# A decoder layer on one core: the output projection of batch 0 spread over the self-attention cycles in halves, and its transposed rows passed through a score bank

## The chip, the cores and the metric

One core of one Trainium2 chip runs the whole layer. The metric is the device time of one execution in microseconds; less is better. TensorE is called PE in the profile, VectorE DVE, ScalarE ACT, GpSimd POOL, and SP is the engine that issues the DMAs.

## The reference

```
x = layernorm(x + self_attention(x))      # 32 heads of 16, causal, ALiBi bias, softmax, output projection w_proj
x = layernorm(x + cross_attention(x, ctx))# 32 query heads of 128, 8 key/value heads, keys and values of ctx and of x
x = layernorm(x + grouped_ffn(x))         # 16 groups: 32 -> 128, gelu, 128 -> 32
```

x is 2 x 256 x 512 and ctx is 2 x 512 x 512, in float32. So there are 512 tokens of x in four tiles of 128, and for the keys and values of the cross-attention 1536 rows (1024 of ctx and 512 of x) in twelve tiles of 128. The tiles of ctx come first; those of x need the output of the first layer norm.

## The kernel before

Each product in full precision is made of three matmuls, hi x hi, hi x lo and lo x hi (`three_passes`, lines 48 to 50): whatever goes into such a product is split by ACT, which makes the hi part, and DVE (or POOL), which subtracts to get the lo part. The program has three stages. The change is in the first, `self_attention_and_keys`, which does the self-attention and, between its pieces, the key and value projections of the cross-attention.

The self-attention runs in 16 quads of four heads (8 quads for batch 0, then 8 for batch 1). A quad's scores, S, are one set of 16 small matmuls into banks 0 to 3, a bank for each head. E is a head's softmax: DVE adds the bias and takes the extreme (line 588, semaphore `s_out`), ACT makes the exponentials (448). R, for half a quad, is the reciprocals (DVE, 597), the scaling of the probabilities (POOL, 383 and 385) and the bias of the next quad (POOL, 378). T is a head's three transposes on PE (810) and their copy out by DVE (603). Every second quad, PV weighs the values with two quads of probabilities (822), and A splits the result: ACT (455), then DVE (609, semaphore `at_lo`).

The filler between these is the projection of the twelve row tiles. `part (n, r)` is a pair of the four contraction steps of a group, six matmuls of 128 x 512: each row tile n has 8, two for each of its four groups (keys 0, keys 1, values 0, values 1), and the groups take banks 5 and 6 in turn. ACT copies a key group out and squares it (478, 483), DVE sums the squares (626, 629), POOL scales the rows (411, 413), PE turns them (KT, 839) and ACT copies them out for the store (KX, 462). CT turns the rows of ctx (832).

At the end of a batch, Y is the output projection of a token tile in two halves of six matmuls each, into bank 5 or 6. LN is its sum with x and the statistics on DVE (672 to 678, semaphore `y_sum` after the sum) and a power on POOL (430). X1 normalises on DVE (686). XT turns the rows (PE 898, ACT 541, DVE 681, semaphore `x1t_lo`), and the key tiles 8 to 11 are projected from these.

The order of all this is one list, `order_of_work`, written out by hand: a loop over c, in the following called cycle c, which does S of quad c + 1, E and R of quad c + 1 and T of quad c. Every engine walks the same list and does its own share of each entry, so the list is the order on each engine. T, PV, CT, KT, XT and QT use banks 4 and 7 in turn (`RING`), so each of them waits (`drained`) until the last but one of them has been taken out.

On PE, cycles 8 to 14 read, with p for part:

```
8   S9 PV3 p5.0 T8.0 KT4.0 p5.1 Y0.0 Y0.1 Y1.0 Y1.1 T8.1 p5.2 T8.2 KT4.1 p5.3 T8.3 p5.4
9   S10 CT6 p5.5 T9.0 p5.6 T9.1 p5.7 XT0 T9.2 p6.0 XT1 T9.3 KT5.0 p6.1
10  S11 PV4 p6.2 T10.0 KT5.1 p6.3 T10.1 p6.4 T10.2 CT7 p6.5 T10.3 p6.6
11  S12 p6.7 T11.0 p7.0 T11.1 KT6.0 p7.1 T11.2 p7.2 T11.3
12  S13 PV5 KT6.1 p7.3 T12.0 p7.4 T12.1 p7.5 T12.2 p7.6 T12.3
13  S14 p7.7 T13.0 p8.0 T13.1 KT7.0 p8.1 T13.2 p8.2 T13.3
14  S15 PV6 KT7.1 p8.3 T14.0 p8.4 T14.1 p8.5 T14.2 p8.6 T14.3
```

On DVE, LN 0 stands between the copy of T8.1 and E9.2 in this list, LN 1 between the copy of T8.2 and E9.3.

Of the kernel before, what the change touches and what calls it, by code (L numbers as in the profile page):

```python
# [81 lines left out]
def order_of_work():  # L82

    order = [("S", 0), ("W", 5), ("V", 0), ("E", (0, 0)), ("V", 1), ("E", (0, 1)), ("V", 2), ("E", (0, 2)), ("CT", 0), ("CX", 0), ("V", 3),
             ("E", (0, 3)), ("R", (0, 0)), ("W", 6), ("R", (0, 1))]
    q = 0

    def parts(count):
        nonlocal q
        for _ in range(count):  # L90
            n, r = divmod(q, PARTS)
            if r in (1, 3) and n >= 1:
                order.append(("KT", (n - 1, r // 2)))
            if r == 5 and n + 1 < B * CT:
                order.append(("CT", n + 1))
            order.append(("part", (n, r)))
            if r in (1, 3) and n >= 1:
                order.append(("KX", (n - 1, r // 2)))
            if r == 5 and n + 1 < B * CT:
                order.append(("CX", n + 1))  # L100
            q += 1

    for c in range(NQ):
        more, pair, mid = c + 1 < NQ, c % 2 == 0 and c >= 2, c - NQ // 2
        if more:
            order.append(("S", c + 1))
        if pair:
            order.append(("PV", c // 2 - 1))
        for i in range(QUAD):
            if mid == 0 and i == 1:  # L110
                parts(q % 2)
                order += [("Y", (0, 0)), ("Y", (0, 1)), ("Y", (1, 0)), ("Y", (1, 1))]
            elif mid == 0 and i >= 2:
                order.append(("LN", i - 2))
                parts(1)
            elif mid == 1 and i < 2:
                order.append(("X1", i))
                parts(1)
            elif mid == 1:
                parts(1)  # L120
                order.append(("XT", i - 2))
            else:
                parts(2 if c == NQ - 1 and i == 0 else 1)
            if more:
                order.append(("E", (c + 1, i)))
            if pair and i == 0:
                order.append(("A", c // 2 - 1))
            if i == 3 and more:
                order.append(("R", (c + 1, 0)))
            order.append(("T", (c, i)))  # L130
        if c < NQ - 5:
            parts(1)
        if c == 3:
            order.append(("W", 7))
        if more:
            order.append(("R", (c + 1, 1)))
    parts(1)
    order += [("PV", NQ // 2 - 1), ("A", NQ // 2 - 1)]
    parts(1)
    order += [("Y", (2, 0)), ("Y", (2, 1))]  # L140
    parts(1)
    order.append(("LN", 2))
    parts(1)
    order += [("X1", 2), ("Y", (3, 0)), ("XT", 2), ("Y", (3, 1)), ("LN", 3)]
    parts(1)
    order.append(("W", 8))
    parts(1)
    order.append(("X1", 3))
    parts(2)
    order += [("Q", 0), ("XT", 3)]  # L150
    parts(1)
    order += [("Q", 1), ("QM", (0, 0))]
    parts(1)
    order.append(("QT", 0))
    parts(1)
    order += [("Q", 2), ("QT", 1)]
    parts(1)
    order += [("Q", 3), ("QM", (0, 1))]
    parts(1)
    order += [("W", 9), ("QM", (1, 0))]  # L160
    parts(1)
    order.append(("KS", 0))
    parts(1)
    for j in range(UT):
        order.append(("XS", j))
        parts(1)
        if j == 0:
            order.append(("QM", (1, 1)))
        order.append(("XM", j))
        if j > 0:  # L170
            order.append(("XI", j - 1))
        order.append(("XE", j))
    parts(1)
    order.append(("XI", UT - 1))
    parts(max(0, ROWS * PARTS - q))
    parts(4)
    order += [("XS", UT), ("XS", UT + 1)]
    parts(1)
    assert q == ROWS * PARTS + 5
    return order  # L180


def self_attention_and_keys(nc, d, k):

    with ExitStack() as ctx:
# [66 lines left out]
        GH = KVH // 2  # L252
        RING, GROUPS = (4, 7), (5, 6)
        before = {4: ("V", 0), 7: ("V", 3), 5: ("V", 1), 6: ("V", 2)}
        place = {}
        for what, a in ORDER:
            if what in ("T", "PV", "CT", "KT", "XT", "QT"):
                at = RING[sum(1 for e in place if e[0] in ("T", "PV", "CT", "KT", "XT", "QT")) % 2]
            elif what == "Y" and a[1] == 0 or what == "part" and a[1] % 2 == 0 and a[0] < ROWS:
                at = GROUPS[sum(1 for e in place if e[0] in ("Y", "part")) % 2]  # L260
            else:
                continue
            place[what, a] = at, before[at]
            before[at] = what, a

        def bank_of(what, a):
            if what == "part":
                a = (a[0], a[1] - a[1] % 2)
            elif what == "Y":
                a = (a, 0)  # L270
            return place[what, a][0]
# [162 lines left out]
        def _(act):  # L434
# [30 lines left out]
            def part(n, r):  # L465
                if r == 0 and n >= 1:
                    act.wait_ge(g_ps, 4 * n)
                    if n >= 2:
                        act.wait_ge(v_store, 16 * (n - 1))
                    nc.scalar.activation(v_st[:, GH:KVH, :].rearrange("p h e -> p (h e)"),  # L470
                                         bank[:, bank_of("part", (n - 1, 6)), :], ACT.Copy).then_inc(vg_late, 1)
                if r in (2, 4) and n < ROWS:
                    g = r // 2 - 1
                    w = slice(GH * g, GH * (g + 1))
                    act.wait_ge(g_ps, 4 * n + g + 1)
                    if n >= 1:
                        act.wait_ge(kt_ps, 2 * n + g - 1)
                    nc.scalar.activation(k_rows[:, w, :].rearrange("p h e -> p (h e)"),
                                         bank[:, bank_of("part", (n, 2 * g)), :], ACT.Copy).then_inc(kg_out, 1)
                    act.wait_ge(kg_out, 2 * n + g + 1)  # L480
                    if 2 * n + g >= 1:
                        act.wait_ge(kss_made, 2 * n + g)
                    nc.scalar.activation(k_sq[:], k_rows[:, w, :], ACT.Square).then_inc(ksq_made, 1)

            for j in range(TT):
                act.wait_ge(xt_ps, j + 1)
# [23 lines left out]
            for what, a in ORDER:  # L510
# [13 lines left out]
                elif what == "W":  # L524
# [7 lines left out]
                        act.wait_ge(q_ps, TT)  # L532
                    for i in range(KT):
                        weights_hi(a, i)
                elif what == "A":
                    attention_hi(a)
                elif what == "part":
                    part(*a)
                elif what == "XT":
# [25 lines left out]
        def _(dve):  # L565
# [87 lines left out]
            for what, a in ORDER:  # L653
# [15 lines left out]
                elif what == "LN":  # L669
# [6 lines left out]
                    nc.vector.bn_aggr(mv[:, a, :], stats[:, a, :]).then_inc(y_mv, 1)  # L676
                    dve.wait_ge(y_mv, a + 1)
                    nc.vector.tensor_scalar(var[:, a:a + 1], mv[:, a, 1:2], LN_EPS, None, ALU.add).then_inc(var_made, 1)
                elif what == "XT":
                    dve.wait_ge(x1t_hi, a + 1)  # L680
                    nc.vector.tensor_tensor(xT_lo[:, :, tokens(a)],
                                            bank[:, bank_of("XT", a), :].rearrange("p (k t) -> p k t", k=KT),
# [46 lines left out]
        def _(pe):  # L729
            def drained(what, a):  # L730

                held, i = place[what, a][1]
                if held == "V":
                    pe.wait_ge(v_out, 2 * (i + 1))
                elif held == "T":
                    pe.wait_ge(pt_out, QUAD * i[0] + i[1] + 1)
                elif held == "PV":
# [50 lines left out]
            def scores(c):  # L788
# [2 lines left out]
                keys = kT_odd if odds else kT_even  # L791
                if c >= 1:
                    pe.wait_ge(s_out, QUAD * c)
                if c < NQ // 2:
                    pe.wait_ge(k_out, m + 1)
                    pe.wait_ge(k_odd_out, m + 1)
# [1069 lines left out]
```

## Time and profile before

| | us |
|---|---|
| median of 3 runs | 865.54 (865.48 to 865.6) |
| the profiled execution, its time | 865.81 |
| the profiled execution, its span | 864.0 |
| PE busy in it | 828.4 |
| DVE, ACT, POOL busy | 548.3, 475.1, 524.4 |
| mean granted clock of PE | 0.991 |

The span is from the first to the last instruction; the execution's own time is 1.8 us longer, and 0.3 us above the median. A busy time is a sum over the span. The ends of matmuls are modelled, and in a stream they overlap: the distance from one start to the next is what a matmul costs there, and a row marks as idle only what lies behind the modelled end.

### The profile page before, as it was taken

The page shows a single profiled execution, that of the slowest core. Times are in us where ns is not written, and L with a number is a line of the kernel's source. Part 1 is how long each engine was busy: PE and PEld are TensorE (multiplying, and loading weights), DVE is VectorE, ACT ScalarE, POOL GpSimd, SP SyncE. Part 2 cuts the span into 40 slices and gives each one's busy share as a digit, 9 for nine tenths or more (in the row PEclk, how much of TensorE's full clock was granted, in tenths as well). Part 3 has the DMA queues.
Part 4 walks back from the last instruction along what each step waited for, and adds up shares of the span by engine and source line. Part 5 has one row for each costly group of instructions (what it writes and reads, how often), then busy time and mean ns, then how long its engine had stood idle before and what let it go on. Part 6 is the DMA issues. An engine that isn't in the chain of part 4 may idle for free. (4 is left out here: it accounts for less than half of the span.)

```text
span 864.0 us, 15103 instructions
## 1 busy us (share of the span) xinstructions
PE 828.4 (96%) x4841; PEld 696.8 (81%) x4841; DVE 548.3 (63%) x1505; ACT 475.1 (55%) x1006; POOL 524.4 (61%) x676
## 2 busy tenths in 40 slices
PE   7999999899999899999999999999999999999976
PEld 5777777677887688888888888888888888888763
DVE  4376665656445667767676776667677767767543
ACT  5666663565345645555555555556555545555363
POOL 3576873676425476666756756775775676446831
PEclk9999999999999999999999999999999999999998
DMA  7604222121141532102112121121121102000011
GB/s 225 185 30 134 63 87 94 53 74 50 49 135 50 170 103 87 50 20 86 46 40 67 36 67 67 36 67 67 36 67 67 36 11 71 1 0 2 0 25 49
DMA packets 48510, 56.22 MB, mean 65 GB/s; under 512 B 4670, under 2 KB 29772, under 8 KB 48460
## 3 DMA queue, kind: packets, MB, share of 16 engines
q1 hardware_dynamic: 48460, 55.59, 20.9%
q8 instruction: 27, 0.44, 0.2%
q14 instruction: 23, 0.19, 0.1%
HBM read 41.95 MB, written 13.63 MB: 64 GB/s over the span
## 5 line engine op out<-in xcount | busy, mean ns | idle before, releaser
L1202 POOL TENSOR_SCALAR prob<-prob,x_rinv 128x768 f32<-128x768 f32 x124 | 113.1, 912 | 175.7 <-DVE x_rinv L1368 175.7
L1310 ACT ACTIVATE pT_hi<-bank 128x512 fp32r<-128x512 f32 x192 | 114.4, 598 | 93.8 <-PE bank L1500 92.7
L1293 ACT ACTIVATE prob<-bank,x_nm,q_rms 128x768 f32<-128x768 f32 x124 | 123.3, 994 | 46.1 <-DVE x_nm L1362 45.8
L1402 DVE TENSOR_TENSOR pT_lo<-bank,pT_hi 128x512 fp32r<-128x512 f32 x192 | 130.3, 680 | 6.9 <-ACT pT_hi L1310 5.4
L1359 DVE TENSOR_REDUCE x_mx<-bank 128x1 f32<-128x768 f32 x124 | 118.3, 954 | 22.8 <-PE bank L1463 22.4
L1500 PE MATMUL bank<-ident,prob 128*128 128x128 f32 x768 | 115.7, 273 | 4.3 <-POOL prob L1202 2.9
L1500 PEld LDWEIGHTS bank<-ident,prob 128*128 128x128 f32 x768 | 95.1, 141 | 16.6 <-POOL prob L1202 3.6
L48 PE MATMUL bank<-pT_hi,xv_hi 128*128 128x512 f32 x192 | 86.5, 450 | 0.9 <-DVE pT_lo L1402 0.8
L448 ACT ACTIVATE s_self<-s_self,nm_self 128x128 f32<-128x128 f32 (+1 forms) x128 | 57.0, 447 | 54.2 <-DVE nm_self L588 54.0
L50 PE MATMUL bank<-pT_hi,xv_lo 128*128 128x512 f32 x192 | 75.7, 394 | 0.0
L49 PE MATMUL bank<-pT_lo,xv_hi 128*128 128x512 f32 x192 | 75.2, 392 | 0.0
L1463 PE MATMUL bank<-xk_hi,qT_hi 128*128 128x384 f32 x244 | 66.0, 352 | 1.1 <-ACT prob L1293 1.0
L1463 PE MATMUL bank<-xk_lo,qT_hi 128*128 128x384 f32 x244 | 63.2, 340 | 0.0
L1463 PE MATMUL bank<-xk_hi,qT_lo 128*128 128x384 f32 x244 | 62.9, 338 | 0.0
L48 PE MATMUL bank<-wq_hi,x_hi 128*128 128x512 f32 x144 | 58.5, 406 | 0.0
L48 PE MATMUL bank<-w_hi,cT_hi 128*128 128x512 f32 x128 | 56.0, 438 | 1.2 <-DVE x_rows L672 1.2
L1319 ACT ACTIVATE oT_hi<-bank 128x512 fp32r<-128x512 f32 x32 | 19.2, 598 | 68.9 <-PE bank L50 68.9
L50 PE MATMUL bank<-wq_hi,x_lo 128*128 128x512 f32 x144 | 56.4, 392 | 0.0
L49 PE MATMUL bank<-wq_lo,x_hi 128*128 128x512 f32 x144 | 56.4, 391 | 0.0
L603 DVE COPY pT_self<-bank 128x384 f32<-128x384 f32 x64 | 35.3, 552 | 30.7 <-PE bank L810 30.5
L48 PE MATMUL bank<-wo_hi,oT_hi 128*128 128x512 f32 x128 | 51.9, 406 | 0.0
L1463 PEld LDWEIGHTS bank<-xk_hi,qT_hi 128*128 128x128 f32 x244 | 43.8, 190 | 9.8 <-ACT prob L1293 2.0
(216 smaller groups left out, 2050.3 us busy)
## 6 DMA issues: line engine op xcount, KB each, us to landing
wo_raw<-in_Wo SPq DMA_DIRECT2D x8, 1024.0 KB, 5.5
v_by_head<-v_st SPq DMA_DIRECT2D x12, 512.0 KB, 3.3
kT_by_head<-kT_st SPq DMA_DIRECT2D x12, 512.0 KB, 3.2
xk_raw<-kT_by_head SPq DMA_DIRECT2D x16, 384.0 KB, 3.2
xv_raw<-v_by_head SPq DMA_DIRECT2D x16, 384.0 KB, 3.2
wq_raw<-in_Wq SPq DMA_DIRECT2D x6, 1024.0 KB, 5.4
wq_raw<-in_w_attn SPq DMA_DIRECT2D x12, 256.0 KB, 3.9
xk_raw<-in_ctx SPq DMA_DIRECT2D x8, 256.0 KB, 2.6
```

The costliest lines, as they stand in the source:

```text
L48: nc.tensor.matmul(out, a_hi, b_hi, start=first, stop=False)
L49: nc.tensor.matmul(out, a_hi, b_lo, start=False, stop=False)
L50: return nc.tensor.matmul(out, a_lo, b_hi, start=False, stop=last)
L448: nc.scalar.activation(s_sb[:, c % 2, i, a:e], s_sb[:, c % 2, i, a:e], ACT.Exp, bias=nm[:, c % 2, i, qt:qt + 1], scale=-1.0, accum_out=rsu ...
L603: nc.vector.tensor_copy(pT[:, c % 2, i, :], bank[:, bank_of("T", (c, i)), 0:3 * P]).then_inc(pt_out, 1)
L1202: nc.gpsimd.tensor_scalar(prob[:, s, :], prob[:, s, :], rinv[:, s:s + 1], 1.0, ALU.mult, ALU.mult)\
L1293: nc.scalar.activation(prob[:, s, :].rearrange("p (a e) -> p a e", a=2), bank[:, at:at + 2, 0:HALF], ACT.Exp, bias=nm[:, s:s + 1], scale=q ...
L1310: nc.scalar.activation(pT_hi[:, a, :], bank[:, turn.bank[s, what, a], :], ACT.Copy)\
L1359: nc.vector.reduce_max(mx[:, s:s + 1], bank[:, at:at + 2, 0:HALF], AX.XY)\
L1402: nc.vector.tensor_tensor(pT_lo[:, a, :], bank[:, turn.bank[s, what, a], :], f32(pT_hi[:, a, :]), ALU.subtract).then_inc(ring_out, 1)
L1463: last = nc.tensor.matmul(bank[:, at + c, 0:HALF], a_hi[:, g, w], k_part[:, b, c * HALF:(c + 1) * HALF], start=start, stop=stop)
L1500: last = nc.tensor.transpose(bank[:, at, j * P:(j + 1) * P], prob[:, UT * (s % 2) + j, a * P:(a + 1) * P], ident[:])
```

## The change

The order of cycles 8 to 14 is another one, and two entries are split. KG, the copy and squaring of a key group on ACT, and AH, ACT's share of A, become entries of their own, and so does XL, DVE's share of XT. KG stands where it stood, ahead of part 2 or 4 of its tile, except that two of them are placed ahead of the Y halves. XT 0 and XT 1 no longer use the ring of banks 4 and 7 but bank 0, once the first head's scores of the quad have been read, and the next quad's scores wait for XL. Cycles 11 to 14 have five parts (a half Y is counted as one), as the others. On PE the new list is:

```
8   S9 PV3 p5.0 T8.0 KT4.0 p5.1 T8.1 Y0.0 T8.2 Y0.1 T8.3 p5.2
9   S10 KT4.1 p5.3 T9.0 Y1.0 T9.1 Y1.1 T9.2 p5.4 T9.3 CT6 p5.5
10  S11 PV4 p5.6 T10.0 p5.7 T10.1 p6.0 XT0 T10.2 KT5.0 p6.1 T10.3 p6.2
11  S12 KT5.1 p6.3 T11.0 p6.4 T11.1 CT7 p6.5 XT1 T11.2 p6.6 T11.3 p6.7
12  S13 PV5 p7.0 T12.0 KT6.0 p7.1 T12.1 p7.2 T12.2 KT6.1 p7.3 T12.3 p7.4
13  S14 p7.5 T13.0 p7.6 T13.1 p7.7 T13.2 p8.0 T13.3 KT7.0 p8.1
14  S15 PV6 p8.2 T14.0 KT7.1 p8.3 T14.1 p8.4 T14.2 p8.5 T14.3 p8.6
```

LN 0 stands ahead of KT4.1 in cycle 9, LN 1 behind part 5.4 and ahead of E10.3, X1 0 and X1 1 in cycle 10, XL 0 and XL 1 behind the copies of T10.3 and T11.3. All entries up to T8.0, KT4.0 and part 5.1 and all from part 8.7 on are as before.

```diff
+    copied = set()
+
+    def copy_keys(n, g):
+
+        if (n, g) not in copied and n < ROWS:
+            copied.add((n, g))
+            order.append(("KG", (n, g)))
+
-    def parts(count):
+    def parts(count, late=None):
+
         nonlocal q
         for _ in range(count):
             n, r = divmod(q, PARTS)
+            if r in (2, 4):
+                copy_keys(n, r // 2 - 1)
             if r in (1, 3) and n >= 1:
                 order.append(("KT", (n - 1, r // 2)))
...
             if r in (1, 3) and n >= 1:
-                order.append(("KX", (n - 1, r // 2)))
+                (order if late is None else late).append(("KX", (n - 1, r // 2)))
...
         for i in range(QUAD):
-            if mid == 0 and i == 1:
+            late = []
+            if mid == 0 and i == 2:
                 parts(q % 2)
-                order += [("Y", (0, 0)), ("Y", (0, 1)), ("Y", (1, 0)), ("Y", (1, 1))]
-            elif mid == 0 and i >= 2:
-                order.append(("LN", i - 2))
+                copy_keys(q // PARTS, q % PARTS // 2 - 1)
+                order.append(("Y", (0, 0)))
+            elif mid == 0 and i == 3:
+                order.append(("Y", (0, 1)))
+            elif mid == 1 and i == 0:
+                order.append(("LN", 0))
                 parts(1)
-            elif mid == 1 and i < 2:
-                order.append(("X1", i))
-                parts(1)
+            elif mid == 1 and i < 3:
+                if i == 1:
+                    copy_keys(q // PARTS, q % PARTS // 2 - 1)
+                order.append(("Y", (1, i - 1)))
             elif mid == 1:
                 parts(1)
-                order.append(("XT", i - 2))
+                order.append(("LN", 1))
+            elif mid == 2 and i in (0, 2):
+                order.append(("X1", i // 2))
+                parts(1)
+            elif pair and i == 0:
+                parts(1, late)
             else:
                 parts(2 if c == NQ - 1 and i == 0 else 1)
+            if late:
+                order.append(("AH", c // 2 - 1))
             if more:
                 order.append(("E", (c + 1, i)))
+            order += late
             if pair and i == 0:
+                if not late:
+                    order.append(("AH", c // 2 - 1))
                 order.append(("A", c // 2 - 1))
+            if mid in (2, 3) and i == 2:
+                order.append(("XT", mid - 2))
             if i == 3 and more:
                 order.append(("R", (c + 1, 0)))
             order.append(("T", (c, i)))
-        if c < NQ - 5:
+            if mid in (2, 3) and i == 3:
+                order.append(("XL", mid - 2))
+        if c < NQ - 1:
             parts(1)
...
+            if what == "XT" and quad < NQ - 1:
+                place[what, a] = 0, ("E", quad)
+                rows_over[quad + 1] = a
+                continue
...
+                elif held == "E":
+                    pe.wait_ge(s_out, QUAD * i + 1)
...
                 if c >= 1:
                     pe.wait_ge(s_out, QUAD * c)
+                if c in rows_over:
+                    pe.wait_ge(x1t_lo, rows_over[c] + 1)
```

On ACT the body of the key copy moves unchanged from `part` into a function `copy_keys`, called for KG.

## Rows read from the trace of the kernel before

**Rows 1.** The page: busy time by engine, share of the span, instructions.
```profile
PE 828.4 (96%) x4841; PEld 696.8 (81%) x4841; DVE 548.3 (63%) x1505; ACT 475.1 (55%) x1006; POOL 524.4 (61%) x676
```

**Rows 2.** Windows, core 0: busy us (instructions) of each engine, granted clock, DMA.
```profile
144.50:166.50 22.00, 17.83 (x110) 13.44 (x110) 16.24 (x53) 10.13 (x33) 11.95 (x22) 1.00 0.20 60
166.50:189.00 22.50, 22.50 (x205) 17.28 (x206) 14.09 (x57) 13.49 (x43) 15.10 (x32) 1.00 0.16 48
227.90:268.80 40.90, 40.79 (x217) 32.77 (x216) 17.69 (x63) 15.16 (x28) 12.08 (x13) 1.00 0.29 88
270.00:275.00 5.00, 4.13 (x16) 3.64 (x17) 3.25 (x6) 0.90 (x3) 4.92 (x5) 0.70 0.05 15
```

**Rows 3.** Timeline of PE: start, us, idle before and its releaser.
```profile
144.48 0.49 PE L810 MATMUL bank<-ident,s_self 128*128 128x128 f32 x3
146.21 0.50 PE L48 MATMUL bank<-w_hi,cT_hi 128*128 128x512 f32 x1 [1.25 <-DVE x_rows L672]
...
158.18 0.60 PE L898 MATMUL bank<-ident,x_rows 128*128 128x128 f32 x4
159.30 0.52 PE L810 MATMUL bank<-ident,s_self 128*128 128x128 f32 x3 [0.52 <-DVE pT_self L603]
...
161.12 0.63 PE L898 MATMUL bank<-ident,x_rows 128*128 128x128 f32 x4
162.13 0.52 PE L810 MATMUL bank<-ident,s_self 128*128 128x128 f32 x3 [0.39 <-DVE pT_self L603]
164.44 0.63 PE L839 MATMUL bank<-ident,k_rows 128*128 128x128 f32 x4 [1.78 <-DVE x_lo L681]
...
189.08 0.48 PE L48 MATMUL bank<-w_hi,cT_hi 128*128 128x512 f32 x1
...
191.95 0.52 PE L810 MATMUL bank<-ident,s_self 128*128 128x128 f32 x3 [1.23 <-DVE x_lo L609]
...
197.86 0.94 PE L800 MATMUL bank<-kT_even,qT 32*128 32x128 f32 x16 [0.22 <-DVE nm_self L588]
```

**Rows 4.** Timeline of PE where nothing is waited for.
```profile
154.73 0.49 PE L810 MATMUL bank<-ident,s_self 128*128 128x128 f32 x3
154.97 0.48 PE L48 MATMUL bank<-w_hi,cT_hi 128*128 128x512 f32 x1
155.29 0.39 PE L49 MATMUL bank<-w_lo,cT_hi 128*128 128x512 f32 x1
155.52 0.40 PE L50 MATMUL bank<-w_hi,cT_lo 128*128 128x512 f32 x1
...
156.45 0.49 PE L810 MATMUL bank<-ident,s_self 128*128 128x128 f32 x3
...
237.76 0.60 PE L898 MATMUL bank<-ident,x_rows 128*128 128x128 f32 x4
238.12 0.48 PE L48 MATMUL bank<-wq_hi,x_hi 128*128 128x512 f32 x1
```

**Rows 5.** Timeline of DVE around the layer norm and the first rows turned.
```profile
145.00 0.56 DVE L603 COPY pT_self<-bank 128x384 f32<-128x384 f32 x1 [6.56 <-PE bank L810]
145.48 0.68 DVE L672 TENSOR_TENSOR x_rows<-bank,x_rows 128x512 f32<-128x512 f32 x1
...
147.26 0.29 DVE L588 CUSTOM_DVE_ANT_0 s_self<-bank,alibi 128x128 f32<-128x128 f32 x1
...
163.60 0.69 DVE L681 TENSOR_TENSOR x_lo<-bank,x_hi 128x512 fp32r<-128x512 f32 x1 [1.61 <-ACT x_hi L541]
```

**Rows 6.** Lines of POOL, 133 to 230 us: busy, mean ns, idle.
```profile
L413 POOL TENSOR_TENSOR k_rows<-k_rows,k_inv 128x512 f32<-128x512 f32 x9 | 9.4, 1042 | 0.7
L411 POOL TENSOR_TENSOR k_inv<-k_ms,minus_half 128x4 f32<-128x4 f32 x9 | 9.1, 1014 | 13.4 <-DVE k_ms L629 13.2
L430 POOL TENSOR_TENSOR rstd<-var,minus_half 128x1 f32<-128x1 f32 x2 | 1.1, 560 | 12.7 <-DVE var L678 12.7
```

**Rows 7.** Timeline of PE at the end of the stage.
```profile
270.87 0.59 PE L926 MATMUL bank<-xk_hi,qT_hi 128*128 128x384 f32 x2 [1.82 <-issue]
```

More of the change, by code:

```diff
@@ L137, in order_of_work @@
     parts(1)
-    order += [("PV", NQ // 2 - 1), ("A", NQ // 2 - 1)]
+    order += [("PV", NQ // 2 - 1), ("AH", NQ // 2 - 1), ("A", NQ // 2 - 1)]
     parts(1)
@@ L143, in order_of_work @@
     parts(1)
-    order += [("X1", 2), ("Y", (3, 0)), ("XT", 2), ("Y", (3, 1)), ("LN", 3)]
+    order += [("X1", 2), ("Y", (3, 0)), ("XT", 2), ("XL", 2), ("Y", (3, 1)), ("LN", 3)]
     parts(1)
@@ L149, in order_of_work @@
     parts(2)
-    order += [("Q", 0), ("XT", 3)]
+    order += [("Q", 0), ("XT", 3), ("XL", 3)]
     parts(1)
@@ L254, in self_attention_and_keys @@
         before = {4: ("V", 0), 7: ("V", 3), 5: ("V", 1), 6: ("V", 2)}
-        place = {}
+        place, quad, rows_over = {}, 0, {}
+        ring_uses = 0
         for what, a in ORDER:
+            if what == "S":
+                quad = a
+            if what == "XT" and quad < NQ - 1:
+                place[what, a] = 0, ("E", quad)
+                rows_over[quad + 1] = a
+                continue
             if what in ("T", "PV", "CT", "KT", "XT", "QT"):
-                at = RING[sum(1 for e in place if e[0] in ("T", "PV", "CT", "KT", "XT", "QT")) % 2]
+                at = RING[ring_uses % 2]
+                ring_uses += 1
             elif what == "Y" and a[1] == 0 or what == "part" and a[1] % 2 == 0 and a[0] < ROWS:
@@ L471, in part, with copy_keys @@
                                          bank[:, bank_of("part", (n - 1, 6)), :], ACT.Copy).then_inc(vg_late, 1)
[L472 to L483, printed above, removed]
+            def copy_keys(n, g):
+                w = slice(GH * g, GH * (g + 1))
+                act.wait_ge(g_ps, 4 * n + g + 1)
+                if n >= 1:
+                    act.wait_ge(kt_ps, 2 * n + g - 1)
+                nc.scalar.activation(k_rows[:, w, :].rearrange("p h e -> p (h e)"),
+                                     bank[:, bank_of("part", (n, 2 * g)), :], ACT.Copy).then_inc(kg_out, 1)
+                act.wait_ge(kg_out, 2 * n + g + 1)
+                if 2 * n + g >= 1:
+                    act.wait_ge(kss_made, 2 * n + g)
+                nc.scalar.activation(k_sq[:], k_rows[:, w, :], ACT.Square).then_inc(ksq_made, 1)
             for j in range(TT):
@@ L534, in _ @@
                         weights_hi(a, i)
-                elif what == "A":
+                elif what == "AH":
                     attention_hi(a)
+                elif what == "KG":
+                    copy_keys(*a)
                 elif what == "part":
@@ L678, in _ @@
                     nc.vector.tensor_scalar(var[:, a:a + 1], mv[:, a, 1:2], LN_EPS, None, ALU.add).then_inc(var_made, 1)
-                elif what == "XT":
+                elif what == "XL":
                     dve.wait_ge(x1t_hi, a + 1)
```

## The prediction

> **What bounds the kernel now.** I read the page first: PE is busy for 828.4 of 864.0 us, and the next engine, DVE, for 548.3 [rows 1]. The kernel is PE's list of work, and a new order, which leaves the same matmuls to do, can gain only where PE stands still. The windows say where that is. In each row the first figure is the length, then comes PE's busy time; the granted clock is the third figure from the end. PE stands for 4.2 of the 22 us from 144.5, not at all in the next 22.5, and for 0.1 us from 227.9 to 268.8 [rows 2]; what lies behind that the change doesn't touch. Then I went through PE's timeline from 133 us (S9, the first entry of cycle 8) to 227.9 us and looked for starts that stand further apart than the same pair does elsewhere.
>
> The measure for that is a stretch without waits: from the start of three transposes T to the part behind them 0.24 us, from the start of a part's six matmuls to the next T 1.48, from the four transposes of XT to a product 0.36 [rows 4]. Against it, the places that I find in cycles 8 to 14 are:
> - T8.1 to part 5.2: 1.73 for 0.24, that is 1.5 lost. Part 5.2 goes to the bank of Y0, which DVE gives back with the sum (672), and the sum stands behind the copy of T8.1, which PE did only after all four Y halves. DVE had been idle for 6.56 us by then [rows 3, 5].
> - XT0 and XT1 to the next T: 1.12 and 1.01 for 0.36, so 0.8 and 0.6 lost, and T9.3 to KT5.0 another 1.8 by the row's own idle time. All three wait for the ring of two banks [rows 3].
> - part 7.3 to T12.0: 2.87 for 1.48, so 1.4 lost. T12.0 uses the bank of PV5, two ring entries back, and waits for A5. Part 8.3 to T14.0 repeats it with the same 2.87.
> - S14 waits 0.2 for the last head's scores to be read, and S10 the same [rows 3].
>
> The sum is 1.5 + 0.8 + 0.6 + 1.8 + 1.4 + 1.4 + 0.2 + 0.2 = 7.9 us. This is what the change can save at most, but for a few tenths of hidden distance.
>
> **The change, part by part.**
>
> *Y in halves between transposes.* In cycle 8 a Y half stands behind T8.1 and T8.2 each, and the layer norm is moved to where Y0 is complete. From the copy of T8.1 on, DVE has its copies and E9.2, E9.3 every 1.7 us in place of one gap of 6.56. Part 5.2 no longer follows Y0 in the same bank: it takes that of part 5.0, for which KG 5.0 is now in front of Y0.0, and ACT is idle enough to make it there (10.13 of 22 us busy) [rows 2]. Y1.0 needs the sum of LN 0, which comes a part, KT4.1, S10 and a T earlier. So the 1.5 goes. The cost is in the number of unbroken runs of products, since Y halves in a row saved restarts. Counting in the two lists, PE goes from 31 unbroken runs of products to 35. A restart costs about 0.1 us: the first matmul of a part is 0.32 us from the next, where the two after it are 0.23 apart [rows 4]. Four of them: 0.4 us.
>
> The Trainium skill (TensorE: Matmul & The Clock Gate, LDWEIGHTS) puts a weight load at the number of columns over 1.2 GHz, 0.107 us for 128, which would make the four restarts 0.43 us if each lays one load bare; the sum stays as it is with either.
>
> *XT through bank 0.* Both XT leave the ring, so T10.2 follows XT0 without the ring's wait, and KT5.0 no longer follows XT1's neighbours: 0.8 + 0.6 + 1.8 go. What is new is a wait of S12 for XL 0 and of S13 for XL 1. Behind the waiting S stands all of PE's list, and DVE's next scores with it. XL stands behind the copy of T10.3. That copy starts 0.52 after the transposes start (144.48 to 145.00), the next DVE instruction follows 0.48 later, XL takes 0.69, and the release reaches PE 0.15 after its end (163.60 + 0.69 to 164.44) [rows 3, 5]: 1.84 us. PE has 0.24 + 1.48 = 1.72 of cover, T10.3 and part 6.2. So 0.1 each at best. If DVE is behind at that point by one value copy of the tile (0.7), it is 0.8. I take 0.3 for each: 0.6. If the cover were gone altogether, each would cost 1.8.
>
> *Ring.* In cycles 12 and 14 no KT and no KX stand between PV and T any more, so T12.0 and T14.0 take a bank that is long free. The next ring entry needs A5: in cycle 12 it is KT6.0, a part and a T (1.72) behind PV5, where T12.0 stood a KT and a part behind it (0.4 + 1.48 = 1.9). That is no more cover than before, but ACT reaches its share sooner, by one KX copy of 0.7, and E13.0 no longer stands behind a key sum on DVE. I leave 0.2 of the 1.4 in each of the two cycles, and put 0.4 for cycle 10, where X1 0 and a value copy stand in front of E11.0 and A4, which T10.1 waits for. Together 0.8; at worst the full 1.4 stays in each of the two, 2.8.
>
> *Five parts in cycles 11 to 14, and a part behind every last T.* They only move; the 0.2 + 0.2 of S14 and S10 are then covered by a part. PE's work in all is the same, and everything from part 8.7 on is as before.
>
> *KG, AH.* KG is the same two ACT instructions at the same place but for the two ahead of Y; ACT has the room named above. The branch with `late` needs a part 1 or 3 at the head of an even cycle; in the new list these are 1.2, 2.4, 3.6, 5.0, 5.6, 7.0 and 8.2, so KX is never put behind E. Cost and gain are nil.
>
> *DMAs.* The stores and the load of ctx tile 7 keep their order in SP's queue, and each store still has several us until the staging tile is written again. Nothing is issued more.
>
> *Other engines' load.* Cycle 9 is the dense one. POOL has there one quad (11.0 us for 28 instructions after the two key groups are taken out of the 15.10 of the second window, 12 of them to a quad: 4.7), two key groups at 2.06 and two powers at 0.56 each: 9.9 us [rows 2, 6], against 10.0 for PE's own list (five times 1.48, four T at 0.24, KT and CT at some 0.36 each, S at 0.9). DVE has both layer norms at 1.78 (145.48 to 147.26) [rows 5], 3.6, and the rest of a dense cycle, 14.09 of 22.5 us in the second window or 6.3 in 10: 9.9 as well. Cycles 8 and 10 have no key group, so both engines can catch up, and S11 has two parts between it and LN 1's start. I count 0 for this, at worst 1.4.
>
> The sum: 7.9 saved, less 0.4, 0.6 and 0.8, is 6.1 us. The profiled execution took 865.8, which gives 859.7; the median is 0.3 below it, so 859.4.
>
> *Behind the stage.* The gain is kept only if what follows moves up with PE. To 268.8 PE has no idle time to lose; the wait of 1.82 at 270.87 is for the keys' split on DVE, behind a load whose stores and copies all hang on PE's own list [rows 2, 7], so it moves too. After this pause the granted clock is 0.70 from 270 to 275 [rows 2]: part of that stretch is at 1.2 GHz, the rest at 2.4. A part's six matmuls at the low level, each 0.23 us longer at half the clock, make 1.4 us; that is how far this place can vary either way.
>
> The Trainium skill (TensorE: Matmul & The Clock Gate, the part on the clock gate) says that the monitor's window runs free of the kernel. By it the low stretch could begin or end elsewhere when the pause comes 6 us sooner; the forecast has it the same, and the 1.4 us is in the range.
>
> **The rivals.**
> - *Most is given back inside the stage*: DVE, dense in cycle 9 and with XL in cycles 10 and 11, becomes what PE waits for: 1.4 behind LN 1, 0.8 at S12 and at S13, 2.8 in the ring. That leaves 7.9 - 0.4 - 5.8 = 1.7 to 4.5: 861.0 to 863.8. For it speaks that the cover of XL is short by 0.1 on paper; against it that DVE was busy for only 14.09 of 22.5 us in dense cycles [rows 2].
> - *No change*: PE is early at the handover and waits there for keys and weights as much longer. Then 865.5 within 0.2% (1.7 us). Against it: that load's last condition is the store of tile 9, whose parts PE does in the unchanged list.
> - *Slower*: S12 and S13 wait for a chain, not for an instruction. XL needs ACT's copy, which stands behind E11.2, which needs the bias from POOL, which stands behind R10, and this behind the power of LN 1 and DVE's. If POOL's 9.9 us in a cycle of 10 don't fit, each head's softmax comes late, and every quad after it. It decides the sign when the waits at the two S pass 7.9 - 0.4 = 7.5 us, over 3.7 at each, and can be told from no change at 867.3, 9.3 us of waits; I put its middle at 869. POOL's spare time in cycle 10 speaks against it.
>
> **How the numbers follow.** The likeliest case, 4.5 to 8.2 us saved, is 857.3 to 861.0, and I give it 0.65. Given back in most: 0.18. More than that saved, with the clock's help: 0.03. No change: 0.08. Slower: 0.06. The range 857.0 to 863.2 holds the first and most of the second. A measurement of this kernel can tell about 0.2%, 1.7 us, from no change; so faster by more than that 0.86, the same 0.08, slower 0.06.
>
> **What would show it.** In the changed profile, PE's start-to-start from T8.1 on should be 0.24, then 1.48; no wait of PE for the sum of LN, no wait in the ring around XT; T12.0 and T14.0 right behind their part. S12 and S13 should show an idle time for XL of 0.1 to 0.8 us. S15 should start some 6 us earlier, less what its place in the list shifts, PV7 6 us earlier at about 221.8 (227.9 before), and the first row of the cross-attention's scores at 264.8 (270.87 before). It is wrong if PE waits for DVE by more than 2 us in cycles 9 to 11, if PV7 is early and the scores are not, or if T or KT behind PV still waits over 1 us.

## The result, and the profile after

| | us |
|---|---|
| kernel before, median of 4 runs | 865.57 (865.48 to 866.11) |
| changed kernel, median of 4 runs | 857.17 (855.89 to 858.31) |
| ratio, 95% interval | 0.9896 (0.9871 to 0.9921) |
| the profiled execution of the changed kernel, its time and span | 855.89, 854.1 |

By the ratio this is 856.6 us, 9.0 below the kernel before, where 6.1 were forecast. The median itself, 857.17, is just inside the range. In two other sets of runs the changed kernel gave 0.9879 (0.9851 to 0.9908) and 0.9883 (0.9854 to 0.9912), and a third kernel that came out as the same program (late_xl, below) 0.9867 (0.9846 to 0.9889). By these ratios it is 9 to 11.5 us faster, at and beyond the fast end of the predicted range. One execution of xt_in_ring (2909.98 us) and one of the kernel before (2776.77 us), both in the experiments below, were in a slow state and are left out of the medians and ratios.

The page of the profile shows the same numbers of instructions and less idle time of PE (compare [rows 1]):

```profile
PE 825.4 (97%) x4841; PEld 695.7 (81%) x4841; DVE 547.7 (64%) x1505; ACT 475.8 (56%) x1006; POOL 524.2 (61%) x676
```

The windows of the changed kernel, from S9 on (length, then busy us of PE, PE's weight loads, DVE, ACT, POOL; the granted clock is third from the end). They answer to [rows 2]:

```profile
132.60:154.10 21.50, 21.50 (x165) 16.63 (x164) 13.98 (x56) 11.95 (x40) 12.49 (x29) 1.00 0.22 67
154.10:176.40 22.30, 22.30 (x173) 17.44 (x172) 16.77 (x60) 14.53 (x47) 16.95 (x32) 1.00 0.19 56
176.40:219.60 43.20, 43.20 (x315) 33.97 (x316) 22.71 (x84) 25.14 (x71) 26.84 (x52) 1.00 0.24 72
219.60:260.50 40.90, 40.79 (x217) 32.73 (x216) 17.74 (x63) 15.21 (x28) 12.03 (x13) 1.00 0.29 87
```

From S9 on to PV7 (the first three rows) PE doesn't stand at all by these rows. PV7 starts at 219.56, for 227.92 before. Since S9 started at 132.63 for 133.00, the stretch S9 to PV7 went from 94.92 to 86.93 us: 8.0 saved. What lies between PV7 and the first score row of the cross-attention is as long as before, 42.96 for 42.95, so nothing is given back at the handover.

PE's timeline of the changed kernel at the places of [rows 3]:

```profile
138.65 0.49 PE L854 MATMUL bank<-ident,s_self 128*128 128x128 f32 x3
138.90 0.47 PE L48 MATMUL bank<-wq_hi,x_hi 128*128 128x512 f32 x1
...
142.08 0.49 PE L854 MATMUL bank<-ident,s_self 128*128 128x128 f32 x3
142.33 0.47 PE L48 MATMUL bank<-w_hi,cT_hi 128*128 128x512 f32 x1
...
161.33 0.60 PE L942 MATMUL bank<-ident,x_rows 128*128 128x128 f32 x4
161.77 0.49 PE L854 MATMUL bank<-ident,s_self 128*128 128x128 f32 x3
162.10 0.60 PE L883 MATMUL bank<-ident,k_rows 128*128 128x128 f32 x4
...
163.94 0.49 PE L854 MATMUL bank<-ident,s_self 128*128 128x128 f32 x3
...
165.77 0.94 PE L844 MATMUL bank<-kT_even,qT 32*128 32x128 f32 x16
...
180.16 0.49 PE L854 MATMUL bank<-ident,s_self 128*128 128x128 f32 x3
180.64 0.63 PE L883 MATMUL bank<-ident,k_rows 128*128 128x128 f32 x4
...
262.52 0.58 PE L970 MATMUL bank<-xk_hi,qT_hi 128*128 128x384 f32 x2 [1.82 <-issue]
```

Part 5.2 starts 0.25 us after T8.3 (142.08 to 142.33), T10.2 0.44 after XT0 and KT5.0 0.33 after T10.2. T12.0 to KT6.0 is 0.48 for 0.33 elsewhere: 0.15 us is all that is left of the waits in the ring. The pause in front of the first score row is 1.82 us as in [rows 7].

All starts of PE from S9 to PV7 can be added up in the same way, each kind of step at its usual distance. PE's list without waits comes to 86.5 us before and 86.6 after, of 94.9 and 86.9 measured. So the waits went from some 8.4 us to 0.3, and the new order made the list itself longer by 0.1. Of the 8.4, 8.1 stand at the places that the prediction names, and the rest, like most of the 0.3, is hundredths spread over some 300 starts.

S12 starts at 165.77. DVE's timeline just ahead of it:

```profile
164.47 0.56 DVE L643 COPY pT_self<-bank 128x384 f32<-128x384 f32 x1 [0.97 <-PE bank L854]
164.94 0.68 DVE L721 TENSOR_TENSOR x_lo<-bank,x_hi 128x512 fp32r<-128x512 f32 x1
```

T10.3 starts at 163.94, the copy 0.53 later, XL 0 ends at 165.62, and S12 starts 0.15 after that, 1.83 us after T10.3. The prediction had worked out 1.84. But a part in front of S takes some 0.1 more than one in front of T. Where S follows a part with no XL in play, it takes 1.56 and 1.57 (142.33 to 143.89 and 152.49 to 154.06), and in front of S12 and S13 1.59. So PE comes to S12 just then: the wait is within 0.03 us, and there is no cover to spare.

The profiled execution gained 9.9 us of span. The other part, beyond S9 to PV7, is 0.4 before S9, which the change doesn't touch, and 1.6 from the first score row to the first transposes of the next stage: 16.70 before, 15.08 after. PE's list is the same there. Before, the clock behind the pause was at the lower level (0.70 in the last window of [rows 2]). After, it was not. The same pause, then, and another clock. The second pause of the handover, 2.04 us at 302.74 before and 2.08 at 292.77 after, had a low stretch behind it in both profiles. The windows of the changed kernel around both pauses:

```profile
262.00:265.00 3.00, 2.48 (x14) 2.31 (x15) 1.55 (x3) 0.69 (x1) 3.00 (x3) 1.00 0.00 0
265.00:268.00 3.00, 3.00 (x16) 2.59 (x15) 2.59 (x6) 1.36 (x3) 2.17 (x3) 1.00 0.58 178
291.00:294.00 3.00, 1.23 (x5) 1.23 (x6) 0.93 (x2) 0.60 (x2) 2.92 (x4) 0.84 0.33 62
294.00:297.00 3.00, 3.00 (x13) 2.65 (x12) 2.11 (x4) 1.11 (x2) 2.83 (x5) 0.60 1.03 387
```

### The profile page after: what moved, and what is told of

The parts are those of the page before. It is cut to its first block and busy times, and to the rows that moved or that the text cites. A ratio compares the mean times of both kernels' runs of the same rounds, so it can differ in the third digit from the quotient of the medians.

```text
span 854.1 us, 15105 instructions
## 1 busy us (share of the span) xinstructions
PE 825.4 (97%) x4841; PEld 695.7 (81%) x4841; DVE 547.7 (64%) x1505; ACT 475.8 (56%) x1006; POOL 524.2 (61%) x676
## 5 line engine op out<-in xcount | busy, mean ns | idle before, releaser
L48 PE MATMUL bank<-pT_hi,xv_hi 128*128 128x512 f32 x192 | 86.5, 450 | 0.9 <-DVE pT_lo L1446 0.8
```

The costliest lines, as they stand in the source:

```text
L48: nc.tensor.matmul(out, a_hi, b_hi, start=first, stop=False)
```

## The experiments

Times of whole runs scatter by 4 us for the changed kernel and by 7 us for the kernel before, so the experiments are read from their profiles, in two distances on PE: from S9 to the first score row of the cross-attention (A), and from there to the first transposes of the next stage (B). The last column says how often the clock fell in A. The sets of runs were taken on different chips, each with its own runs of the kernel before, to which the ratio is: the first row and the second are one set, after_again to t_first another (kernel before 866.37), three_edits to keys_first a third (867.76 by its ten other executions), and xl_twice, keys_squares_first and after_third a fourth (866.65). The two distances are taken within one profile each.

| kernel | A | B | median us | ratio to before (95%) | low clock in A |
|---|---|---|---|---|---|
| before | 137.87 | 16.70 | 865.57 | | none |
| changed | 129.89 | 15.08 | 857.17 | 0.9896 (0.9871 to 0.9921) | none |
| after_again | 129.94 | 15.11 | 856.01 | 0.9879 (0.9851 to 0.9908) | none |
| ring_only | 137.40 | 15.12 | 862.35 | 0.9960 (0.9939 to 0.9981) | none |
| kt_behind | 137.71 | 15.12 | 863.87 | 0.9972 (0.9951 to 0.9993) | once |
| t_first | 136.33 | 16.67 | 864.15 | 0.9978 (0.9959 to 0.9997) | none |
| three_edits | 134.32 | 15.11 | 861.46 | 0.9928 (0.9909 to 0.9947) | none |
| xt_in_ring | 136.04 | 15.09 | 859.88 | 0.9912 (0.9893 to 0.9931) | once |
| late_xl | 129.90 | 15.10 | 856.28 | 0.9867 (0.9846 to 0.9889) | none |
| keys_first | 127.88 | 18.79 | 857.76 | 0.9889 (0.9871 to 0.9908) | none |
| xl_twice | 131.21 | 16.69 | 859.13 | 0.9912 (0.9877 to 0.9947) | none |
| keys_squares_first | 127.94 | 15.50 | 853.90 | 0.9868 (0.9839 to 0.9897) | none |
| after_third | 129.91 | 15.11 | 855.87 | 0.9883 (0.9854 to 0.9912) | none |

A repeats within 0.05 us where nothing in it is changed: the four profiles of the changed program, late_xl (below) among them, lie at 129.89 to 129.94.

**The changed kernel again**, as it is.

> The changed kernel unchanged, timed again, because its four runs lay between 855.9 and 858.3 us where those of the kernel before lay within 0.6. If the gain is 8.0 us in cycles 8 to 14 and the rest is the clock behind the pause at the handover (the first row of the cross-attention's scores), the profile shows PV7 at 219.6 again within 0.4, and the time from that first score row to the first transposes of the next stage differs from the 15.1 us of the first profile by the length of the low-clock stretch there, up to 1.6. If the gain itself varies, PV7 moves. Time 856 to 858.5.

Measured: A 129.94, B 15.11. PV7 starts at 220.36, 0.8 later than in the first profile and outside the 0.4 expected, but S9 starts 0.74 later too: from S9 to PV7 it is 86.99 for 86.93. The gain in the stage is fixed, and the scatter comes from three other places. Over all thirteen profiles S9 starts between 131.7 and 134.8 us, and no run shows why. B is 15.1 or 16.7 in all but the two kernels that change the handover. And what lies behind B is 576.2 to 576.5 us in the six profiles with a low stretch behind the second pause of the handover, and 574.8 to 575.2 in the seven without.

**XT through score banks, in the old order.** Each XT of cycle 9 takes a bank whose scores have been read:

```diff
+            if what == "XT" and quad < NQ - 1:
+                place[what, a] = a, ("E", (quad, a))
+                rows_over[quad + 1] = a
+                continue
```

> The kernel before, with one part of the change: XT 0 and XT 1 go through the score banks 0 and 1 of the quad whose scores have been read, nothing is reordered. If the waits found in the timeline are each the price of their own place (theory: separate waits), the 0.8, 0.6 and 1.8 us around XT go and nothing comes in their place: 862.3. If PE was held there by DVE and POOL being behind (rival: one common lag), T9.2, T9.3 or S11 wait in their place and it stays above 864.

Measured: A fell by 0.5 us, not by 3.2. The time of 862.35 hits the 862.3 of separate waits for another reason: in the profile B was 15.12 for 16.70, and no low stretch came behind the second pause either. The waits of PE in cycles 9 and 10:

```profile
160.87 0.63 PE L851 MATMUL bank<-ident,k_rows 128*128 128x128 f32 x4 [0.88 <-DVE pT_self L611]
163.63 0.94 PE L812 MATMUL bank<-kT_odd,qT 32*128 32x128 f32 x16 [0.73 <-DVE nm_self L596]
...
168.77 0.63 PE L851 MATMUL bank<-ident,k_rows 128*128 128x128 f32 x4 [0.86 <-DVE x_lo L617]
```

The waits for the ring are gone around XT, and in their place KT5.0 waits for a copy, S11 for the last scores to be read and KT5.1 for A4, all of them DVE. DVE was late in the old cycle 9, whatever the bank. That was the rival. But it was not late by its load alone. From 151 to 157 us it is full (5.01 of 6.00), and from 157.0 to 163.6, where PE stands, it is busy for only 3.87 of 6.60 and waits itself, for ACT's copy of the turned rows:

```profile
151.00:157.00 6.00, 6.00 (x45) 4.75 (x42) 5.01 (x16) 3.35 (x11) 5.62 (x12) 1.00 0.16 50
157.00:163.60 6.60, 5.01 (x31) 3.88 (x29) 3.87 (x18) 3.42 (x11) 2.87 (x4) 1.00 0.11 34
```

```profile
159.01 0.69 DVE L689 TENSOR_TENSOR x_lo<-bank,x_hi 128x512 fp32r<-128x512 f32 x1 [1.12 <-ACT x_hi L549]
162.33 0.69 DVE L689 TENSOR_TENSOR x_lo<-bank,x_hi 128x512 fp32r<-128x512 f32 x1 [1.60 <-ACT x_hi L549]
160.35 0.40 ACT L456 ACTIVATE s_self<-s_self,nm_self 128x128 f32<-128x128 f32 x1 [1.37 <-DVE nm_self L596]
```

That copy stands behind a head's exponentials on ACT, these wait for DVE's scores of the head, and the scores stand on DVE behind the last XL. So it is a chain that goes to and fro between the two engines, with XL ahead of the next head's scores. The change takes XL out of it, to a place behind the copy of T10.3; none of the edits alone does.

**KT behind T at the head of cycles 12 and 14**, in the old order:

```diff
+            elif mid in (4, 6) and i == 0:
+                parts(1, turned)
...
             order.append(("T", (c, i)))
+            order += turned
```

> The kernel before, with one part of the change: at the head of cycles 12 and 14 the key transposes and their copy stand behind T12.0 and T14.0 in place of ahead of part 7.3 and 8.3. Separate waits: the two waits of 1.4 us go, but the KT that now follows T uses the bank of PV and may keep 0.2 of each: 863.1. Common lag: KT or T12.1 waits as long as T12.0 did, over 864.5. A theory on ACT's side (the KX copy ahead of the exponentials makes A late) expects the same as separate waits; it is told apart in a later run.

Measured: from S13 to S14 10.73 for 11.49, from S15 to PV7 20.76 for 21.67, so 0.8 and 0.9 gone of the 1.4 each, where 1.2 each was expected. Part of the rest is with the KT, which now waits 0.43 for A5 and 0.29 for A6:

```profile
194.11 0.63 PE L848 MATMUL bank<-ident,k_rows 128*128 128x128 f32 x4 [0.43 <-DVE x_lo L618]
```

The whole of A fell by only 0.2, because cycle 9, where this kernel is as before, took 1.4 us more. The windows show where: the pauses around XT were followed by a stretch at the lower clock, which the profile of the kernel before did not have there. The median, 863.87, lies between the two theories.

```profile
163.00:166.00 3.00, 0.83 (x7) 0.42 (x5) 1.39 (x6) 1.95 (x6) 0.00 (x0) 1.00 0.13 42
166.00:169.00 3.00, 3.00 (x10) 2.25 (x10) 1.03 (x5) 1.56 (x5) 2.32 (x6) 0.52 0.43 133
```

**T8.1 ahead of the Y block**, in the old order:

```diff
-                order += [("Y", (0, 0)), ("Y", (0, 1)), ("Y", (1, 0)), ("Y", (1, 1))]
...
             order.append(("T", (c, i)))
+            if mid == 0 and i == 1:
+                order += [("Y", (0, 0)), ("Y", (0, 1)), ("Y", (1, 0)), ("Y", (1, 1))]
```

> The kernel before, with T8.1 and its copy ahead of the four Y halves in a row, which stay in a row. Separate waits: DVE no longer stands for 6.6 us, the sum of Y0 is done while Y1 runs, the wait of part 5.2 goes and one restart is added: 1.5 less 0.1, 864.1; the waits around XT stay. Common lag: the 6.6 us in which DVE had nothing to do were what made it late around XT and at the head of cycle 12 too, then it gives 3 us or more, 862.5 or less.

Measured: cycle 8 took 17.47 for 18.97, 1.5 less, and A fell by 1.5. The waits around XT stayed as they were. So this one is a wait of its own, and its price was right. The 6.56 us that DVE stood idle ahead of it are not what makes it late around XT.

**All three together**, nothing else reordered.

> The kernel before with the three parts tried alone (XT through score banks, KT behind T in cycles 12 and 14, T8.1 ahead of the Y block), and no other reordering. S9 to PV7 took 94.9 us before, 86.9 after the change. Alone the three saved 0.5, 0.9 plus 0.8, and 1.6 of that stretch. Theory now: around XT it is DVE's lag in cycle 9 that PE waits for, whatever the bank, so without spreading the layer norms, X1 and XT over cycles 8 to 11 the three give 3.8 together, 91.1, and a time of 861. Rival, separate waits: with T8.1 first DVE enters cycle 9 early, and 3.2 around XT go too: 88.0 and 858.5.

Measured: A fell by 3.6 us, just what the three gave alone (0.5, 1.7 without the low clock, 1.5), and 4.4 less than the change. S9 to PV7 is 91.36 and the median 861.46, as the theory had it (91.1 and 861). PE waits 0.89, 0.73 and 0.84 us for DVE in cycles 9 and 10, the same three places as in ring_only.

**The spread order, with XT back in the ring** and XL right behind XT:

```diff
-                order.append(("XT", mid - 2))
+                order += [("XT", mid - 2), ("XL", mid - 2)]
...
-            if mid in (2, 3) and i == 3:
-                order.append(("XL", mid - 2))
...
-            if what == "XT" and quad < NQ - 1:
-                place[what, a] = 0, ("E", quad)
-                rows_over[quad + 1] = a
-                continue
```

> The changed kernel with XT 0 and XT 1 in the ring of banks 4 and 7 again, XL right behind XT, the spread order kept. Theory, the spreading of work does it: KT5.0 and T11.3 wait for XL a little, 0.5 us in all, S9 to PV7 87.5. Rival, the score bank does it: KT5.0 and the T behind XT1 wait 1 us or more each as T9.3 and KT5.0 did, 89 to 90, and the time is 2 to 3 us above the changed kernel's.

Measured: A 136.04, 6.1 us more than the change. Cycle 10 took 15.73 for 11.71, cycle 11 11.78 for 10.60 and cycle 12 12.73 for 11.81. S9 to PV7 is 93.08, where the theory had 87.5 and the rival 89 to 90. The theory fell, and the loss is larger than the rival's too. KT5.0 waits for XL, which waits for ACT's copy behind a softmax (1.59 us of DVE's idle time), and behind this pause the clock is low again:

```profile
161.81 0.49 PE L848 MATMUL bank<-ident,s_self 128*128 128x128 f32 x3
164.60 0.63 PE L877 MATMUL bank<-ident,k_rows 128*128 128x128 f32 x4 [2.30 <-DVE x_lo L715]
```

```profile
162.00:165.00 3.00, 0.70 (x8) 0.49 (x6) 1.41 (x5) 1.53 (x6) 0.00 (x0) 1.00 0.56 175
165.00:168.00 3.00, 3.00 (x14) 2.43 (x12) 0.84 (x6) 2.45 (x7) 2.17 (x6) 0.67 0.00 0
```

With some 1.5 us of this put down to the clock, an estimate from the 1.4 to 1.6 of the other low stretches, going back to the ring costs 4.6 us in the spread order, where the bank alone gave 0.5 in the old one. The spread order with the ring gives 3.3 (137.87 less 136.04 and 1.5), the bank without the order 0.5, both 8.0. But the 4.6 are not the bank's alone: in the ring KT5.0 needs XL to be done, so XL can't stand behind the copy of T10.3 there and is moved ahead of it. How much is the bank and how much XL's place was not separated, and neither was the score bank with a late XL in the old order tried.

**XL later on DVE.**

```diff
-            if mid in (2, 3) and i == 3:
-                order.append(("XL", mid - 2))
         if c < NQ - 1:
             parts(1)
+        if mid in (2, 3):
+            order.append(("XL", mid - 2))
```

> The changed kernel with XL 0 and XL 1 one place later on DVE, behind the part and the reciprocals R11.1 and R12.1. In the changed kernel XL 0 ended 0.15 us before S12 could start, with no cover to spare. If S waits for XL as the prediction had it, S12 and S13 start some 0.7 us later each, S9 to PV7 88.3. If the next quads' softmax chain is tight too, each 0.7 is lost a second time in T or PV, 89.7. If the wait costs nothing because the other engines are behind anyway, 86.9.

Parts 6.2 and 6.7, which XL was moved behind, have nothing for DVE, and R11.1 and R12.1 stood still further back. So DVE's list came out as it was, and the run says nothing of XL: it is one more of the changed kernel (A 129.90, none of the three expectations tested).

**XL twice.** So the price was doubled instead:

```diff
+                    if a < 2:
+                        nc.vector.tensor_tensor(xT_lo[:, :, tokens(a)], ...
+                        dve.wait_ge(xl_twice, a + 1)
```

> The changed kernel with XL 0 and XL 1 done twice on DVE, one behind the other (0.69 us more each; the second takes the place of the first's result). If S12 and S13 hang on XL with no cover, as the 1.84 against 1.84 in the changed kernel's trace says, each starts 0.7 us later and S9 to PV7 is 88.3 (86.9 without). If the next quads' softmax is tight behind it, S9 to PV7 reaches 89 or more. If XL has cover after all, 86.9.

```profile
167.22 0.94 PE L850 MATMUL bank<-kT_even,qT 32*128 32x128 f32 x16 [0.67 <-DVE x_lo L727]
178.55 0.94 PE L850 MATMUL bank<-kT_odd,qT 32*128 32x128 f32 x16 [0.68 <-DVE x_lo L727]
```

S12 and S13 wait 0.67 and 0.68 for it, S9 to PV7 is 88.26 (88.3 expected), and A grew by 1.3. The wait is real, PE pays for XL's length one to one, and nothing behind it comes on top.

**The handover: the keys' split first.** On the changed kernel, `KS` ahead of `W 9`:

```diff
-    order += [("Q", 3), ("QM", (0, 1))]
+    order += [("Q", 3), ("QM", (0, 1)), ("KS", 0)]
...
-    order.append(("KS", 0))
```

> The changed kernel with the first keys' split (ACT's two copies, DVE's two subtractions) ahead of the last weights' split at the end of the stage. If the pause of 1.8 us before the first score row is the wait for this split and the low clock behind it follows the pause, the pause goes, the row starts 1.8 us earlier after the same PV7, PE stays at 2.4 GHz in the stretch behind it, and the time is 1.8 to 3.4 us below the changed kernel's, 853 to 854.5. Rival: the row then waits for another input (the square sums, the transposed queries) and the pause only changes its name, within 0.3 of the changed kernel.

Measured: A fell by 2.0, but B grew by 3.7, and the time is 857.76, outside the 853 to 854.5 expected and 1.5 above late_xl, the changed program on the same chip. So the pause was the keys' split, and PE comes to the first score row that much earlier. But the pause moved two score rows on, to the wait for the first exponentials, with the low clock behind it. This is nearer the rival, the pause that only changes its name:

```profile
270.12 0.62 PE L969 MATMUL bank<-xk_hi,qT_hi 128*128 128x384 f32 x2 [1.97 <-ACT prob L599]
```

ACT waits there, by way of DVE, for the second half of the square sums' power on POOL, which stood behind the four subtractions of W 9:

```profile
260.80 5.11 POOL L459 TENSOR_TENSOR wq_lo<-wq_raw,wq_hi 128x512 fp32r<-128x512 f32 x4 [7.48 <-ACT wq_hi L474]
265.87 1.63 POOL L455 TENSOR_TENSOR q_inv<-q_ms,minus_half 128x8 f32<-128x8 f32 x1
```

**The keys' split and the power first:**

```diff
-    order += [("Q", 3), ("QM", (0, 1))]
+    order += [("Q", 3), ("QM", (0, 1)), ("QM", (1, 0)), ("KS", 0)]
...
-    order += [("W", 9), ("QM", (1, 0))]
+    order += [("W", 9)]
...
-    order.append(("KS", 0))
```

> The changed kernel with the first keys' split and the second half of the square sums' power both ahead of the last weights' split. In the run with the keys' split alone PE reached the first score row 2.0 us earlier and stood 2.0 us before the third, for ACT's first exponentials; these wait for the power on POOL, which stood behind four subtractions of 5.7 us. Theory: with the power ahead of them that wait goes too, PV7 to the first score row is 41.0, from there to the next stage's first transposes at most 15.1, and the gain on the changed kernel is 2 us, more where a low-clock stretch behind the pause is spared. Rival: POOL's subtractions now hold the scaling of the first probabilities, and the pause comes back at the next stage's first transposes: 0 to 0.5 us of gain.

```profile
266.88 0.61 PE L969 MATMUL bank<-xk_hi,qT_hi 128*128 128x384 f32 x2 [0.23 <-ACT prob L599]
```

A is 127.94 and B 15.50: 1.6 us less than the changed kernel of the same chip in the profiles, 2.0 in the medians (853.90 for 855.87). B was expected at 15.1 at most; 0.4 of the 2.0 gained in A is given back in it, 0.23 of that in the wait shown. The ranges of the runs overlap (853.08 to 855.56 and 854.75 to 856.88), so the profiles carry this more than the times.

**The changed kernel a third time**, as the measure of these two.

> The changed kernel as it is, on the same chip as the other two, as their measure and as one more profile for the low-clock stretches: S9 to PV7 86.9 and PV7 to the first score row 42.95 as in the two profiles before; low-clock stretches of some 3 us, 1.5 us lost in each, behind none, one or both of the pauses at the handover, and never between S9 and PV7, where PE has no pause any more.

Measured: A 129.91, B 15.11, no low clock in either.

## Why the prediction missed by a little

- *What bounds the kernel* was right. PE's list was the kernel, the gain in the stage came only out of PE's idle time, and it moved through the handover unchanged.
- *The waits found in the timeline*, 7.9 us, were all there, and some 0.5 short: by the sum over all starts it was 8.4. In front of KT5.0 it was 1.99 for the 1.8 of the row's own idle time, and 0.29 at S10 and S14 for 0.2.
- *The restarts*, put at 0.4, cost 0.1. Up to PV7 it is three more unbroken runs and not four, since parts 8.6 and 8.7 now follow each other, and three starts of S right behind a T (0.42 us each) are gone.
- *The step that failed is a size: the waits that the new order would bring.* They were put at 0.6 for XL and 0.8 in the ring, 1.4 in all, and measured within 0.03 at each S and 0.15 at KT6.0, 0.3 in all with the hundredths over the rest. That is 1.1 of the 1.9 us between the 6.1 forecast and the 8.0 measured; the restarts are 0.3, the waits found 0.5. The chain of XL had been worked out to 1.84 us against 1.83 measured, but the forecast added 0.2 to each for a DVE that would be late, and it wasn't. The cover it was held against was 0.1 short, as it took a part in front of T for one in front of S. In the ring, 0.2 was left standing at each of T12.0 and T14.0 and 0.4 put for T10.1. Of these nothing was measured: PE's row at T10.1 (159.59) shows no wait. KX is no longer in front of A, which the prediction itself had named, but no run shows that this is what did it.
- *The range* left too little room at its fast end. It has the clock as 1.4 us either way around 859.4, but 7.9 us saved with the clock on its good side is 856.2, below the 857.0 where the range ends.
- *The load of cycle 9* was put at 9.9 us each for DVE and POOL, of 10. Measured are 7.94 and 6.75 of 10.17 (S10 to S11), so the danger that two of the rivals rest on was overrated.
- *The price of XT through the bank*, 3.2 us, came out, but not by the mechanism named. Alone the bank gave 0.5 (ring_only), since PE then waited for DVE, and DVE in turn for ACT, in the chain through XL. It took the new order as well, with XL behind the copy of T10.3. The rival *most is given back inside the stage* describes ring_only and three_edits; it does not describe the change.
- *The order alone* would not have done it either: xt_in_ring keeps it but for XL's place, and loses 4.6 us and a stretch of the clock.
- *Handover*: no loss, as forecast. The clock was named as 1.4 us either way, and the profiled execution had 1.6 of that on its good side. By the ratios the change gave 9.0 to 11.5 us where A gives 8.0. That the clock makes up the rest is borne out by the mean granted clock of every run: 0.9909 over 29 runs of the kernel before and 0.9947 over six of after_again on the same chip, 0.9905 and 0.9952 on the chip of after_third, 0.9900 and 0.9940 on that of late_xl. The differences are 3.3 to 4.1 us of full clock in 866, an upper estimate of what the low stretches cost, against 2.1 to 3.5 of rest. Where in the run they fall these figures don't say. One place is shown: of the four kernels that still have a pause of 1.8 to 2.3 us in front of KT5.0 (before, kt_behind, t_first, xt_in_ring), two had a low stretch behind it in the one profile taken, at a cost of 1.4 us in kt_behind, and the changed kernel has no pause there. On one chip the kernels with that pause, kt_behind and t_first, have a mean clock of 0.9921 and 0.9924, and ring_only, whose longest wait there is 0.88 us, has 0.9945. On another, xt_in_ring with 0.9938 and three_edits with 0.9933 don't show this. What stays open is how often the clock falls there, and why S9 moves by 3.1 us between executions.
- *The rivals* of no change and of a slower kernel did not come about. POOL, at 16.95 of 22.3 us in the dense windows, never held PE.

## What to carry to other kernels

Sum the start-to-start excess on the bound engine, and then follow each wait one step further back: was its releaser held by one thing only, or does it stand in a chain that goes on without the thing you move? A place's price can be had alone only in the first case (T8.1 here, 1.5 of 1.5). In the second, moving a bank gave 0.5 of 3.2 us, and the rest came only with the new order, in which the subtraction XL no longer stands ahead of the next head's scores. The releaser's own idle time says whether it is held or overloaded: DVE was busy for 3.87 of 6.60 us where PE waited for it, so there it was held. For a new wait, a chain worked out to a tenth of a microsecond from rows can be trusted; a surcharge for lateness should come from a row that shows the engine late at that place. When a pause is taken away in front of a queue of dependants, look which of them needs something that stood behind the thing moved, as the power did behind the weights' split.

## What the runs showed of the hardware

A short pause of PE can be followed by some 3 us in which the granted clock is at 0.5, that is at the lower of its two levels, and costs 1.2 to 1.6 us. It doesn't follow each time: behind the pause of 1.82 us in front of the first score row it came in 3 of 11 profiles (B 16.67 to 16.70 in place of 15.1), behind those in front of KT5.0 in 2 of 4, and behind the second pause of the handover (2.03 to 2.08 us) in 6 of 13. Further on, behind a pause of 3.33 to 3.34 us in front of the turned rows (L1690 before, L1734 after), it came in all 13. For one and the same program these stretches alone move the time by some us. The Trainium skill (TensorE: Matmul & The Clock Gate, the part on the clock gate) has the monitor's window run free of the kernel, which fits that the same pause has it in one execution and not in another; no run here shows the window itself.
